# One PSUM bank moved from row maxima to scores in a self-attention loop

## The chip, the cores and the metric

The kernel runs on one core of a Trainium2 chip. The metric is the device time of one execution in microseconds (us), lower is better.

## What is computed

A decoder layer on `x` of 2 x 2048 x 512 in float32: self-attention with 16 heads of 32, then a cross-attention on a short context, then a mixture of eight experts, each with a residual and a layer norm. The change is in the self-attention:

```
qkv = x @ qkv_w + qkv_b                      # (2, 2048, 3, 16, 32)
attn = einsum('bnhd,bmhd->bhnm', q, k) * scale
attn = softmax(attn, axis=-1)
out = einsum('bhnm,bmhd->bnhd', attn, v) @ proj_w + proj_b
```

## The kernel before

The self-attention works on units (one batch and a group of four heads, 8 units) and in each on 4 chunks of 512 queries: 32 chunks. A chunk goes over 16 tiles of 128 keys (`kt`). For each key tile and head there is one *slot*: 64 per chunk, 2048 in all, with `CHUNKS` = 32, `T` = 16 and `HG` = 4 heads.

A slot has two matmuls on TensorE:

- the maxima pass (`max_pass`, L574): queries of the *next* chunk against 512 keys, one bank `mx` of 128 x 512. VectorE reduces it to a maximum per row (`reduce_max`, L463). The maxima of a chunk are ready before its scores start; the passes run 12 slots ahead beyond that.
- the score (`score`, L620): keys against the queries of this chunk, one bank `sc`. ScalarE makes the exponential of it (L426) into SBUF.

The order of the work is written out by hand for each engine, and semaphores hold the engines together. On TensorE a slot is always `max_pass`, then `score`:

```
for i in range(HG):
    n = (g + 1) * NMAX + LEAD + kt * PER_STEP + i
    if n < CHUNKS * NMAX:
        max_pass(n, n % NMAX, n // NMAX)
    score(g, kt, i)
    if i == 1 and kt % 2 == 0:
        burst(g, kt)
    if i == 2 and kt == T - EARLY and g + 1 < CHUNKS:
        transpose_shift(g + 1)
if (g, kt) in PART_AT:
    project_part(*PART_AT[g, kt])
```

`burst` is the products of probabilities with values (L589, `sa_pv`) of the two key tiles before, at every even key tile after its second slot, with the row sums (L597, `sa_den`) every fourth tile. `project_part` (L561, L565, `sa_misc`) is a piece of the next unit's projection, after key tiles 0 to 11. So TensorE's slots lie in runs: two slots, a piece of projection, the four slots of the odd key tile, a piece of projection, two slots, a burst. Without projection (tiles 12 to 15, and nearly everywhere in the last unit) eight slots follow each other between two bursts.

VectorE has, between the reductions and in its own written order, the reciprocals of the row sums (L490, at tiles 3 and 4), the leaving of a projection's result (L444, L455, L457, at tiles 4, 8 and 12), the shifts for the next chunk after tile 12 (`make_shift`: L468, L472, L474) and their leaving (L481) at tile 14, after TensorE has transposed them (L581) in tile 13. GpSimd adds the probabilities of four key tiles pairwise (L247), some 2.4 us each. The last chunk and the last 12 slots of the one before it have no maxima passes left.

PSUM has eight banks, all of them used here: two `sc`, three `mx`, and one each for `pv`, `den` and `misc`. The transposes at the start of the kernel also use `sc[0]` and `sc[1]`; that is not changed.

Of the kernel before, what the change touches and what calls it, by code (L numbers as in the profile page):

```python
# [10 lines left out]
ACT = mybir.ActivationFunctionType  # L11
AX_X = mybir.AxisListType.X

P = 128
BANK = 512
# [56 lines left out]
def self_attention(nc, z, x, xT_dram, qkv_w, qkv_b, attnT_dram, rows_dram):  # L72

    B, N, C, KC, G, HG, D, T, NQ = z.B, z.N, z.C, z.KC, z.G, z.HG, z.D, z.T, z.NQ
    SCALE = float(D) ** -0.5
    UNITS = B * G
    CHUNKS = UNITS * NQ
    QK = 3 * D
    AUG = QK + 2
# [66 lines left out]
    with ExitStack() as ctx:  # L146
        s = Stage(nc, ctx, "sa")
# [8 lines left out]
        q_stack = s.sb("q_stack", [P, HG, N], F32R)  # L156
        k_stack = s.sb("k_stack", [P, 2, HG, N], F32R)
        v = s.sb("v", [P, 2, T, P])
        prob = s.sb("prob", [P, 4, HG, BANK])
        part_max = s.sb("part_max", [P, TQ, HG, KQ])  # L160
# [6 lines left out]
        recip = s.sb("recip", [P, 2, BANK])  # L167
        empty = s.sb("empty", [P, W])

        sc = [s.ps(f"sc{i}") for i in range(2)]  # L170
        mx = [s.ps(f"mx{i}") for i in range(3)]
        pv = s.ps("pv")
        den = s.ps("den")
        misc = s.ps("misc")
# [12 lines left out]
        max_mm, max_read = s.sem("max_mm"), s.sem("max_read")  # L187
        top_ready, shift_hi, shift_ready = s.sem("top_ready"), s.sem("shift_hi"), s.sem("shift_ready")
        shift_mm, shiftT_ready, shift_in = s.sem("shift_mm"), s.sem("shiftT_ready"), s.sem("shift_in")
        sc_mm, prob_ready = s.sem("sc_mm"), s.sem("prob_ready")  # L190
# [11 lines left out]
        def after(engine, sem, value):  # L202

            if value > 0:
                engine.wait_ge(sem, value)
# [17 lines left out]
        @block.gpsimd  # L223
        def _(pool):
            make_ident(pool, ident, ident0, ident_ready)
            pool.wait_ge(ident_ready, 1)
            pool.memset(empty[:, :], 0.0).then_inc(made, 1)
            pool.wait_ge(made, 1)
            pool.memset(empty[:, C + 1:W].bitcast(I32), SKIP).then_inc(made, 1)
            for i in SPLITS:  # L230
                if JOBS[i].place is None:
                    move_stack(pool, i, (2, 3), stacked_too)

            def add_step(g, i, k):


                d = g * QUADS + i
                if k == 1:

                    after(pool, den_mm, d - 1)  # L240
                for half in range(2):
                    heads = slice(2 * half, 2 * half + 2)
                    pool.wait_ge(prob_ready, (g * T + 4 * i + k) * HG + 2 * half + 2)
                    if k > 1:
                        pool.wait_ge(quad_ready, d * ADDS + 2 * (k - 1) - 1 + half)
                    so_far = prob[:, 0, heads, :] if k == 1 else quad_sum[:, i % 2, heads, :]
                    pool.tensor_tensor(quad_sum[:, i % 2, heads, :], so_far, prob[:, k, heads, :], ALU.add).then_inc(quad_ready, 1)  # L247

            def divide(g):

                pool.wait_ge(sums_ready, g + 1)
                pool.wait_ge(recip_ready, TQ * (g + 1))
                pool.tensor_tensor(recip[:, g % 2, :], sums[:, :], recip[:, g % 2, :], ALU.mult).then_inc(attn_ready, 1)


            for i in (2, 3):
                pool.wait_ge(out_x[i], 2 * 16)
            for g in range(CHUNKS):
                for i in range(QUADS):
                    for k in range(1, 4):  # L260
                        add_step(g, i, k)
                        if (i, k) == DIVIDE_AT and g > 0:
                            divide(g - 1)
            divide(CHUNKS - 1)
# [88 lines left out]
        @block.scalar  # L353
        def _(act):

            def load_rows(chunk):
                act.dma_start(prob[:, chunk % NQ, :, :], x_v[chunk // NQ, chunk % NQ, :, :, :]).then_inc(in_rows[chunk % NQ], 16)

            def leave_transposes(chunk):

                b, n = chunk // NQ, chunk % NQ
                slot = xT[:, n % 2, :, :] if b == 0 else quad_sum[:, n % 2, :, :]
                if n >= 2:

                    act.wait_ge(out_x[2 * b + n % 2], 16)
                    if b == 0:
                        act.wait_ge(proj_mm, max(i for i, o in enumerate(FIRST_OPS) if o[1] == n - 2) + 1)
                for k in range(KC):
                    i = chunk * KC + k
                    act.wait_ge(tr_mm, i + 1)  # L370
                    act.activation(slot[:, k, :], sc[i % 2][:, :], ACT.Copy).then_inc(tr_read, 1)
                if b + 1 < B:
                    load_rows(chunk + NQ)
                act.wait_ge(tr_read, (chunk + 1) * KC)
                act.dma_start(xT_v[b, :, :, n * BANK:(n + 1) * BANK], slot).then_inc(out_x[2 * b + n % 2], 16)

            def leave_high(i):

                order = SPLITS.index(i)
                act.wait_ge(proj_mm, i + 1)  # L380
                if order >= 2:
                    before = JOBS[SPLITS[order - 2]]
                    stacked_first(act, before.what, before.n)
                bias = qkb[:, 0 if JOBS[i].what == "q" else 1, 0:1]
                act.activation(hilo[:, order % 2, 0, :], first_bank[i % 3][:, :], ACT.Identity, bias=bias).then_inc(hi_ready, 1)

            for chunk in range(NQ):
                load_rows(chunk)
            act.wait_ge(in_b, 16)
            for what, n in ALONE + sum(BETWEEN, []):  # L390
                if what == "t":
                    leave_transposes(n)
                elif what != "v":
                    leave_high(FIRST_OPS.index((what, n)))
            for i in range(4):
                act.wait_ge(out_x[i], 2 * 16)

            def leave_pv(g):

                act.wait_ge(pv_mm, (g + 1) * T)  # L400
                after(act, attn_ready, g)
                act.activation(sums[:, :], pv[:, :], ACT.Copy).then_inc(sums_ready, 1)

            def leave_den(g):

                act.wait_ge(den_mm, (g + 1) * QUADS)
                after(act, recip_ready, TQ * g)
                act.activation(dens[:, :], den[:, :], ACT.Copy).then_inc(dens_ready, 1)  # L408

            for g in range(CHUNKS):  # L410
                for kt in range(T):
                    step = g * T + kt
                    for j in range(HG):
                        n = step * HG + j
                        if j == 2 and kt == SUMS_AT and g > 0:
                            leave_pv(g - 1)
                        if j == 2 and kt == DENS_AT and g > 0:
                            leave_den(g - 1)
                        act.wait_ge(sc_mm, n + 1)

                        if j == 0:
                            after(act, pv_mm, step - 3)
                        if j % 2 == 0 and step >= 4:

                            act.wait_ge(quad_ready, (step // 4 - 1) * ADDS + 2 * max(kt % 4 - 1, 0) + j // 2 + 1)
                        act.activation(prob[:, kt % 4, j, :], sc[n % 2][:, :], ACT.Exp, scale=SCALE).then_inc(prob_ready, 1)  # L426
            leave_pv(CHUNKS - 1)
            leave_den(CHUNKS - 1)

        @block.vector  # L430
        def _(dve):
# [28 lines left out]
            def reduce_max(n, m):  # L460
                dve.wait_ge(max_mm, n + 1)
                q, j, k = m // (HG * KQ), m // KQ % HG, m % KQ
                dve.reduce_max(part_max[:, q, j, k:k + 1], mx[n % 3][:, :], AX_X).then_inc(max_read, 1)  # L463

            def make_shift(g):

# [35 lines left out]
            for m in range(2):  # L502
                reduce_max(NMAX + m, m)
# [4 lines left out]
            for g in range(CHUNKS):  # L508
                for kt in range(T):
                    for i in range(PER_STEP):  # L510
                        n = (g + 1) * NMAX + LEAD + kt * PER_STEP + i
# [14 lines left out]
        def _(pe):  # L526
# [41 lines left out]

            def max_pass(n, m, g):

                after(pe, max_read, n - 2)
                q, j, k = m // (HG * KQ), m // KQ % HG, m % KQ
                at = g % NQ * BANK + q * P
                pe.matmul(mx[n % 3][:, :], q_stack[0:QK, j, at:at + P], k_stack[0:QK, g // NQ % 2, j, k * BANK:(k + 1) * BANK],  # L574
                          start=True, stop=True).then_inc(max_mm, 1)

            def transpose_shift(g):
# [38 lines left out]

            def score(g, kt, j):
                n = (g * T + kt) * HG + j
                after(pe, prob_ready, n - 1)
                pe.matmul(sc[n % 2][:, :], k_stack[0:AUG, g // NQ % 2, j, kt * P:(kt + 1) * P],  # L620
                          q_stack[0:AUG, j, g % NQ * BANK:(g % NQ + 1) * BANK], start=True, stop=True).then_inc(sc_mm, 1)

            pe.wait_ge(ident_ready, 1)
# [25 lines left out]
            for g in range(CHUNKS):  # L649

                pe.wait_ge(shift_in, (g + 1) * 16 * HG)
                for kt in range(T):
# [7 lines left out]
                    for i in range(HG):  # L660
                        n = (g + 1) * NMAX + LEAD + kt * PER_STEP + i
# [1319 lines left out]
```

## Time and profile before

| | |
|---|---|
| median of 3 runs | 3720.26 us (3717.48 to 3720.76) |
| the profiled execution | 3720.95 us |
| its span, first to last instruction | 3719.2 us |
| busy in the span: TensorE matmuls | 3454.1 us (93%) |
| VectorE | 2508.9 us (67%) |
| ScalarE | 1671.8 us (45%) |
| GpSimd | 2053.2 us (55%) |
| mean granted TensorE clock | 0.958 of full |

The span is that of one profiled execution, and all rows are of it. Times in a timeline are from the start of the span. Matmuls are pipelined, and their ends are modelled, so a busy TensorE is not one at its peak: a wait can also stand ahead of a matmul's weight load (PEld), while the matmul before is still shown as busy. The loop over the chunks lies from about 110 to 2196 us of the span; the maxima passes end at 2110.

### The profile page before, as it was taken

What the parts mean: (1) busy time and instruction counts of PE and PEld (TensorE: products, weight loads), DVE (VectorE), ACT (ScalarE), POOL (GpSimd) and SP (SyncE); (2) the same over time, 40 slices, a digit from 0 to 9 for tenths busy, and PEclk for the clock granted to TensorE, in tenths of its full rate; (3) what the DMA queues carried; (4) which work ended last, traced back from release to release, by engine and by line L of the source; (5) the groups of instructions that cost most, each with busy time, mean ns of one, the idle gap of its engine ahead of it and who ended that gap; (6) DMA issues with size and microseconds to landing.
All of it is one profiled execution on the core that took longest, in us unless ns stands there. A gap on an engine that the chain in (4) does not pass through costs nothing. (4 is left out here: it accounts for less than half of the span.)

```text
span 3719.2 us, 50285 instructions
## 1 busy us (share of the span) xinstructions
PE 3454.1 (93%) x18109; PEld 2267.8 (61%) x18109; DVE 2508.9 (67%) x4510; ACT 1671.8 (45%) x3035; POOL 2053.2 (55%) x1025
## 2 busy tenths in 40 slices
PE   7999999999999999999999857999959999999996
PEld 5455455455455454554554325878849889988885
DVE  5777777777777777777777525778744665556667
ACT  2555555555555555555555533334312333223333
POOL 2689888888888888898888860011120011101111
PEclk9999999999999999999999878999969999999998
DMA  6321321312213122223210022122132243223333
GB/s 219 101 58 61 91 66 61 95 49 80 87 49 100 56 66 86 63 72 91 66 43 22 4 90 65 57 93 71 69 122 68 95 135 117 98 84 120 126 114 108
DMA packets 190274, 308.44 MB, mean 83 GB/s; under 512 B 25513, under 2 KB 72233, under 8 KB 190010
## 3 DMA queue, kind: packets, MB, share of 16 engines
q1 hardware_dynamic: 164330, 238.58, 20.6%
q0 software_dynamic: 14592, 44.32, 3.4%
q10 hardware_dynamic: 11088, 22.02, 1.7%
q8 instruction: 166, 2.72, 0.3%
q14 instruction: 98, 0.80, 0.1%
HBM read 195.66 MB, written 61.33 MB: 69 GB/s over the span
## 5 line engine op out<-in xcount | busy, mean ns | idle before, releaser
L463 DVE TENSOR_REDUCE sa_part_max<-sa_mx 128x1 f32<-128x512 f32 x2048 | 1281.6, 679 | 543.0 <-PE sa_mx L574 539.0
L426 ACT ACTIVATE sa_prob<-sa_sc 128x512 f32<-128x512 f32 x2048 | 1121.9, 595 | 823.3 <-PE sa_sc L620 780.5
L247 POOL TENSOR_TENSOR sa_quad_sum<-sa_quad_sum,sa_prob 128x1024 f32<-128x1024 f32 x512 | 1207.3, 2404 | 7.7 <-ACT sa_prob L426 7.7
L574 PE MATMUL sa_mx<-sa_k_stack,sa_q_stack 96*128 96x512 f32 x2048 | 967.0, 474 | 27.1 <-DVE sa_part_max L463 15.9
L620 PE MATMUL sa_sc<-sa_q_stack,sa_k_stack 98*128 98x512 f32 x2048 | 864.9, 424 | 8.2 <-ACT sa_prob L426 8.1
L247 POOL TENSOR_TENSOR sa_quad_sum<-sa_prob 128x1024 f32<-128x1024 f32 x256 | 616.3, 2431 | 257.5 <-ACT sa_prob L426 257.5
L574 PEld LDWEIGHTS sa_mx<-sa_k_stack,sa_q_stack 96*128 96x128 f32 x2048 | 389.5, 190 | 376.8 <-issue 205.5
L620 PEld LDWEIGHTS sa_sc<-sa_q_stack,sa_k_stack 98*128 98x128 f32 x2048 | 389.2, 190 | 318.7 <-ACT sa_prob L426 274.0
L1858 PE MATMUL ex_h<-ex_xT,ex_w 128*128 128x384 f32 (+2 forms) x2688 | 465.7, 329 | 41.6 <-issue 18.0
L589 PE MATMUL sa_pv<-sa_prob,sa_v 128*32 128x512 f32 x4096 | 502.8, 609 | 0.7 <-ACT sa_prob L426 0.7
L1858 PEld LDWEIGHTS ex_h<-ex_xT,ex_w 128*128 128x128 f32 x2688 | 447.7, 195 | 53.5 <-issue 25.4
L1869 PE MATMUL ex_acc<-ex_w,ex_hT 128*128 128x512 f32 x1728 | 418.2, 393 | 2.4 <-DVE ex_hT L1798 2.2
L1869 PEld LDWEIGHTS ex_acc<-ex_w,ex_hT 128*128 128x128 f32 x1728 | 319.1, 188 | 66.7 <-issue 4.9
L1676 POOL DMA_DIRECT2D ex_xg<-rows x48 | 26.5, 557 | 530.4 <-PE ex_h L1837 530.1
L1735 ACT ACTIVATE ex_h<-ex_h,ex_b 128x384 f32<-128x384 f32 x256 | 145.4, 581 | 373.5 <-PE ex_h L1858 373.5
L589 PEld LDWEIGHTS sa_pv<-sa_prob,sa_v 128*32 128x32 f32 x4096 | 108.1, 110 | 246.0 <-issue 241.6
L927 POOL TENSOR_TENSOR ca_rstd<-ca_var_eps,ca_minus_half 128x8 f32<-128x8 f32 x16 | 26.5, 1656 | 394.8 <-DVE ca_var_eps L1010 394.8
L1796 DVE CAST ex_hT<-ex_h 128x384 fp32r<-128x384 f32 x256 | 94.4, 369 | 147.8 <-ACT ex_h L1735 147.4
L1730 ACT ACTIVATE ex_w<-ex_w_in 128x512 fp32r<-128x512 f32 x128 | 80.6, 630 | 217.2 <-PE ex_acc L1869 217.2
L490 DVE RECIPROCAL sa_recip<-sa_dens 128x128 f32<-128x128 f32 x128 | 119.9, 941 | 77.4 <-ACT sa_dens L408 77.4
L1798 DVE TENSOR_TENSOR ex_hT<-ex_h,ex_hT 128x384 fp32r<-128x384 f32 x256 | 142.9, 558 | 8.9
L597 PE MATMUL sa_den<-sa_quad_sum,sa_ones 128*32 128x512 f32 x1024 | 135.4, 601 | 4.5 <-POOL sa_quad_sum L247 4.5
(199 smaller groups left out, 3186.4 us busy)
## 6 DMA issues: line engine op xcount, KB each, us to landing
ex_w_in<-in_L_ffn_w_dram SPq DMA_DIRECT2D x130, 512.0 KB, 4.4
sa_xT<-xT SPq DMA_DIRECT2D x57, 1024.0 KB, 5.1
sa_q_stack<-sa_hilo SPq DMA_DIRECT2D x372, 64.0 KB, 2.0
sa_k_stack<-sa_hilo SPq DMA_DIRECT2D x360, 64.0 KB, 2.0
rows<-sa_empty SPq DMA_DIRECT2D x48, 257.0 KB, 3.8
ex_rows<-rows POOLq DMA_DIRECT2D x8, 1542.0 KB, 7.4
ex_xg<-rows POOLq DMA_DIRECT2D x48, 256.0 KB, 3.0
sa_prob<-in_x_dram ACTq DMA_DIRECT2D x8, 1024.0 KB, 6.9
```

Source lines behind the costliest of these rows:

```text
L247: pool.tensor_tensor(quad_sum[:, i % 2, heads, :], so_far, prob[:, k, heads, :], ALU.add).then_inc(quad_ready, 1)
L426: act.activation(prob[:, kt % 4, j, :], sc[n % 2][:, :], ACT.Exp, scale=SCALE).then_inc(prob_ready, 1)
L463: dve.reduce_max(part_max[:, q, j, k:k + 1], mx[n % 3][:, :], AX_X).then_inc(max_read, 1)
L490: dve.reciprocal(recip[:, g % 2, cols], dens[:, cols]).then_inc(recip_ready, 1)
L574: pe.matmul(mx[n % 3][:, :], q_stack[0:QK, j, at:at + P], k_stack[0:QK, g // NQ % 2, j, k * BANK:(k + 1) * BANK], start=True, stop=True).t ...
L589: last = pe.matmul(pv[D * j:D * (j + 1), :], v[:, buf, kt, D * j:D * (j + 1)], prob[:, kt % 4, j, :], start=(kt == 0), stop=(kt == T - 1))
L597: last = pe.matmul(den[D * j:D * (j + 1), :], ones[:, :], quad_sum[:, d % 2, j, :], start=(d % QUADS == 0), stop=(d % QUADS == QUADS - 1))
L620: pe.matmul(sc[n % 2][:, :], k_stack[0:AUG, g // NQ % 2, j, kt * P:(kt + 1) * P], q_stack[0:AUG, j, g % NQ * BANK:(g % NQ + 1) * BANK], st ...
L1735: act.activation(h[:, j % 2, half * HALF:(half + 1) * HALF], h_bank[half][:, 0:HALF], ACT.Gelu, bias=b1[:, step:step + 1]).then_inc(h_read ...
L1798: dve.tensor_tensor(hT[:, j % 2, 1, cols], h[:, j % 2, cols], hT[:, j % 2, 0, cols].bitcast(F32), ALU.subtract).then_inc(hT_ready, 1)
L1858: last = pe.matmul(h_bank[half][:, 0:slots], w1[:, i % 2, pw, k, :], xT[:, e % 2, px, k, half * HALF:half * HALF + slots], start=(part == ...
L1869: last = pe.matmul(acc[t][:, :], hT[:, i % 2, ph, t * P:(t + 1) * P], w2[:, i % 2, pw, :], start=(i == 0 and part == 0), stop=(i == STEPS ...
```

## The change

One PSUM bank goes from the maxima to the scores: three `sc` and two `mx`. The indices and the two waits on TensorE follow from that: a score now waits until the exponential of the score three before it is done (it was two), and a maxima pass until the reduction of the pass two before it is done (it was three). The instructions and their order are the same on every engine; on TensorE the first three waits shift, because the first score that has to wait is the fourth and the first pass that has to wait is the third.

```diff
-        sc = [s.ps(f"sc{i}") for i in range(2)]
-        mx = [s.ps(f"mx{i}") for i in range(3)]
+        sc = [s.ps(f"sc{i}") for i in range(3)]
+        mx = [s.ps(f"mx{i}") for i in range(2)]
...
-                        act.activation(prob[:, kt % 4, j, :], sc[n % 2][:, :], ACT.Exp, scale=SCALE).then_inc(prob_ready, 1)
+                        act.activation(prob[:, kt % 4, j, :], sc[n % 3][:, :], ACT.Exp, scale=SCALE).then_inc(prob_ready, 1)
...
-                dve.reduce_max(part_max[:, q, j, k:k + 1], mx[n % 3][:, :], AX_X).then_inc(max_read, 1)
+                dve.reduce_max(part_max[:, q, j, k:k + 1], mx[n % 2][:, :], AX_X).then_inc(max_read, 1)
...
             def max_pass(n, m, g):
-                after(pe, max_read, n - 2)
+                after(pe, max_read, n - 1)
...
-                pe.matmul(mx[n % 3][:, :], q_stack[0:QK, j, at:at + P], k_stack[0:QK, g // NQ % 2, j, k * BANK:(k + 1) * BANK],
+                pe.matmul(mx[n % 2][:, :], q_stack[0:QK, j, at:at + P], k_stack[0:QK, g // NQ % 2, j, k * BANK:(k + 1) * BANK],
...
             def score(g, kt, j):
                 n = (g * T + kt) * HG + j
-                after(pe, prob_ready, n - 1)
-                pe.matmul(sc[n % 2][:, :], k_stack[0:AUG, g // NQ % 2, j, kt * P:(kt + 1) * P],
+                after(pe, prob_ready, n - 2)
+                pe.matmul(sc[n % 3][:, :], k_stack[0:AUG, g // NQ % 2, j, kt * P:(kt + 1) * P],
```

## Rows read from the trace of the kernel before

**Rows 1.** Costliest groups: busy us, mean ns | idle before, releaser
```profile
L463 DVE TENSOR_REDUCE sa_part_max<-sa_mx 128x1 f32<-128x512 f32 x2048 | 1281.6, 679 | 543.0 <-PE sa_mx L574 539.0
L426 ACT ACTIVATE sa_prob<-sa_sc 128x512 f32<-128x512 f32 x2048 | 1121.9, 595 | 823.3 <-PE sa_sc L620 780.5
```

**Rows 2.** Waits of TensorE's matmuls: us in total, times, longest
```profile
PE sa_mx L574 <- DVE sa_part_max L463: 15.9, 28, 0.8
...
PE sa_sc L620 <- ACT sa_prob L426: 8.1, 29, 0.5
```

**Rows 3.** Waits of TensorE's weight loads: us in total, times, longest
```profile
PEld sa_sc L620 <- ACT sa_prob L426: 274.0, 911, 1.0
...
PEld sa_mx L574 <- DVE sa_part_max L463: 122.3, 339, 1.1
```

**Rows 4.** Timeline, four-slot run, TensorE, VectorE, ScalarE: start us, us
```profile
830.08 0.40 PE L620 MATMUL sa_sc<-sa_q_stack,sa_k_stack 98*128 98x512 f32 x1
830.32 0.40 PE L574 MATMUL sa_mx<-sa_k_stack,sa_q_stack 96*128 96x512 f32 x1
...
830.78 0.39 PE L574 MATMUL sa_mx<-sa_k_stack,sa_q_stack 96*128 96x512 f32 x1
831.16 0.50 PE L620 MATMUL sa_sc<-sa_q_stack,sa_k_stack 98*128 98x512 f32 x1
831.50 0.40 PE L574 MATMUL sa_mx<-sa_k_stack,sa_q_stack 96*128 96x512 f32 x1
...
831.99 0.50 PE L561 MATMUL sa_misc<-sa_wkv,sa_xT 128*128 128x128 f32 x3
...
830.28 2.48 DVE L463 TENSOR_REDUCE sa_part_max<-sa_mx 128x1 f32<-128x512 f32 x4 [0.54 <-PE sa_mx L574]
...
830.51 2.27 ACT L426 ACTIVATE sa_prob<-sa_sc 128x512 f32<-128x512 f32 x4 [0.74 <-PE sa_sc L620]
```

**Rows 5.** Timeline, eight-slot run, tiles 14 to 0, TensorE and VectorE
```profile
821.35 0.50 PE L574 MATMUL sa_mx<-sa_k_stack,sa_q_stack 96*128 96x512 f32 x1
...
826.06 0.64 PE L589 MATMUL sa_pv<-sa_prob,sa_v 128*32 128x512 f32 x4
...
821.89 4.87 DVE L463 TENSOR_REDUCE sa_part_max<-sa_mx 128x1 f32<-128x512 f32 x8 [1.63 <-PE sa_mx L574]
```

**Rows 6.** Timeline, key tile 5 of a chunk, TensorE and VectorE
```profile
848.89 1.02 PE L565 MATMUL sa_misc<-sa_xT,sa_wq 128*128 128x512 f32 x2
...
847.64 1.81 DVE L463 TENSOR_REDUCE sa_part_max<-sa_mx 128x1 f32<-128x512 f32 x3
```

**Rows 7.** Timeline, key tiles 12 to 14, TensorE and VectorE
```profile
815.76 0.40 PE L574 MATMUL sa_mx<-sa_k_stack,sa_q_stack 96*128 96x512 f32 x1
...
816.45 0.60 PE L581 MATMUL sa_misc<-sa_ident,sa_shift 128*8 128x128 f32 x4
...
818.63 1.93 PE L589 MATMUL sa_pv<-sa_prob,sa_v 128*32 128x512 f32 x16
820.38 1.04 PE L597 MATMUL sa_den<-sa_quad_sum,sa_ones 128*32 128x512 f32 x8
...
815.99 3.07 DVE L463 TENSOR_REDUCE sa_part_max<-sa_mx 128x1 f32<-128x512 f32 x5
```

**Rows 8.** Busy time (instructions) by engine, then PEclk, DMA share, GB/s
```profile
120.00:1925.00 1805.00, 1785.78 (x9440) 922.51 (x9442) 1320.67 (x2136) 1004.57 (x1830) 1608.39 (x694) 1.00 0.24 72
2125.00:2160.00 35.00, 31.40 (x113) 9.91 (x113) 3.39 (x4) 18.65 (x36) 28.69 (x13) 0.71 0.02 8
```

**Rows 9.** L472 (ns min/median/max), and its timeline beside GpSimd and TensorE
```profile
L472 DVE TENSOR_SCALAR sa_shift<-sa_top x32: 175/176/4340, 99.1 to 2111.8; 128x16 fp32r<-128x16 f32 x32
...
1980.76 4.12 DVE L472 TENSOR_SCALAR sa_shift<-sa_top 128x16 fp32r<-128x16 f32 x1
...
1982.50 2.35 POOL L247 TENSOR_TENSOR sa_quad_sum<-sa_prob 128x1024 f32<-128x1024 f32 x1
...
1985.15 1.01 PE L581 MATMUL sa_misc<-sa_ident,sa_shift 128*8 128x128 f32 x4 [3.47 <-DVE sa_shift L474]
```

## The prediction

> **What bounds the kernel now.** I began with the costliest groups [rows 1]. The changed banks belong to the self-attention loop: 2048 passes for maxima and 2048 for scores on TensorE, 2048 reductions on VectorE, 2048 exponentials on ScalarE. The reader is to see the mean durations: a reduction takes 679 ns, an exponential 595 ns. Neither says who sets the pace; that is to be read from a timeline.
>
> Next the waits. TensorE's matmuls show hardly any: 15.9 us in total for a maxima bank and 8.1 us for a score bank [rows 2]. Read alone, that says that neither bank matters. But a matmul waits at its weight load, and the loads waited 274.0 us (911 times) for an exponential and 122.3 us (339 times) for a reduction [rows 3]. So banks do hold TensorE up, and the score bank does more often.
>
> How much of this is on the path is read from a run of slots in time (a slot is one maxima pass and one score). After a piece of projection, the four slots of an odd key tile follow [rows 4]. Unhindered, TensorE issues a matmul some 0.235 us after the one before (830.08, 830.32), so the run's first began at 829.85. The third score is late: it starts at 831.16, 0.05 after the first exponential ends (830.51 + 0.60 = 831.11), since only two score banks exist. The next matmul follows 0.34 after it and not 0.235, as its own weight load was not ahead. The run from 829.85 to 831.99 takes 2.14 us where eight issues would be 1.88, so the score banks cost 0.26. Yet VectorE in these four slots is busy without a gap: four reductions in 2.48 us, thus (2.48 - 0.68) / 3 = 0.60 apart, with 0.68 for one. The maxima pass of slot 4 (831.50) needs the reduction of slot 1 alone, as there are three banks.
>
> In runs of eight slots (key tiles 14, 15 and 0, without projection) the reductions go at (4.87 - 0.68) / 7 = 0.60 each as well [rows 5]. VectorE is therefore the slowest engine inside a run, and it catches up while TensorE does value products and projections. Three maxima banks are what lets TensorE leave a run before VectorE has finished it.
>
> **The change, part by part.** No instruction is added, removed or moved on any engine. Two waits change: score n waits for exponential n-3 in place of n-2, and maxima pass n for reduction n-2 in place of n-3.
>
> *The score side.* With three banks score 3 of a run no longer waits, so 0.26 per four-slot run could come back. But the maxima pass stands before its score in TensorE's order, so it has to come in time first.
>
> *The maxima side, four-slot run* [rows 4]. Reduction 1 ends at 830.28 + 0.68 = 830.96, reduction 2 at 830.88 + 0.68 = 831.56. Maxima pass 3 (now at 830.78) can start 0.05 after the former, 831.01, and score 3 at 831.35. Pass 4 needs reduction 2, 831.61, after that its score at about 831.90, and the projection at 832.15 to 832.2 in place of 831.99: **+0.2 us**. The wait for a score bank is gone and one for a maxima bank stands in its place, and the last slot now has a matmul more behind the wait. Such runs stand alone at key tiles 1, 7, 9 and 11 of each chunk: 4 x 0.2 = 0.8.
>
> *Key tiles 3 to 5.* Here VectorE has four reciprocals of 0.94 us and the projection's result between its reductions, and its queue sets the pace whatever TensorE does. TensorE left the run of tile 5 at 848.89, its last pass having waited for the reduction that ended at 848.27 [rows 6]. With two banks, that reduction lets the pass before it go (848.32), and the last waits for the next one: 848.24 + 0.68 = 848.92, score 849.26, projection 849.49. Against 848.89 that is **+0.6**, tile 3 included, since VectorE's queue is not later.
>
> *Tiles 12 to 14* [rows 7]. Two reductions, then the three small operations that make the shifts, then the others from 815.99. Pass 5 of the run needs reduction 3, which ends at 815.99 + 0.68 = 816.67, in place of reduction 2. It starts at 816.72 (now 815.76). Its score (817.07), the transposes of the shifts at 817.31 (now 816.45) and 0.44 of them, pass 6 at 817.75, pass 7 at 818.22 and pass 8 at 818.92 (reduction 6: 818.18 + 0.68, + 0.05) put the value products at 819.5 in place of 818.63: **+0.9**.
>
> *Tiles 14 to 0* [rows 5]. A late pass, to its reduction 0.54 (821.35 to 821.89), the reduction 0.68, to the next pass in that bank 0.05 to 0.06: 1.28 for two slots, 0.64 each in place of 0.60. Passes 2, 4, 6 and 8 then start at 821.92, 823.22, 824.50 and 825.78; score 8 at 826.12, value products at 826.36 in place of 826.06: **+0.3**.
>
> Sum per chunk 0.8 + 0.6 + 0.9 + 0.3 = 2.6 us; 31 chunks have maxima: **+80.6**. The last three have hardly any projections, so eight-slot runs (0.3) stand where 0.2 stood: +2. Before the loop twelve passes run at VectorE's pace, 12 x 0.04 = 0.5, say +1.
>
> *What comes back.* The last 76 slots have no maxima, and there the third score bank does what it is for. GpSimd's sums of pairs limit that gain: in 2125 to 2160 they leave 35 - 28.7 = 6.3 us [rows 8]. From 0 to 6.3 I take half: -3. And in the last chunks VectorE's operation L472 took 4.12 us in place of 0.18 because it began in the middle of a GpSimd addition; TensorE then stood 3.47 us [rows 9]. A slower TensorE lets GpSimd be less behind, so one of these three collisions may go: -3.5 (bounds: none, -11). By the Trainium skill, SBUF — State Buffer, section Who interferes with whom, a VectorE `tensor_scalar` and a GpSimd operation can hold a shared pair of ports against each other, the second blocked until the first ends. The trace agrees: the operation of 0.18 us ended only when GpSimd's additions did, at 1984.85.
>
> Sum: 80.6 + 2 + 1 - 3 - 3.5 = +77. The profiled execution took 3720.95 (span 3719.2), 0.7 above the median of the runs shown, so the median goes from 3720.3 to about **3798**. Bounds for a chunk: 2.0 if half of tile 12's loss is caught again by the value products' slack, 3.4 if stalls of neighbouring runs add up; that is +62 to +105, and with the last two terms at their ends 3776 to 3820.
>
> **Rivals.** *Faster: the third score bank wins.* For it: 911 waits of weight loads for exponentials against 339 for reductions [rows 3]. If TensorE could start pass 3 before reduction 1 has ended, by a reduction that starts earlier than 0.54 after its pass, the runs would fall to 1.88. It decides at 830.78: reduction 1 would have to end before 830.73, and it ends at 830.96. Price: five four-slot runs of 0.26 per chunk, -1.3 x 31 = -40, 3680. Against it: VectorE's 0.60 per slot. Chance 0.05.
>
> *No change.* A run's later end is taken up by slack behind it. That would need TensorE idle behind a run; instead TensorE is busy 1786 of 1805 us [rows 8], and the value products follow at once. 3720, chance 0.04.
>
> *Slower still: the clock.* In the trace the granted clock is 1.00 from 120 to 1925 and 0.71 from 2125 to 2160, with scores alone in TensorE's slots and after the longest L472, of 4.34 us [rows 8, 9]; that is, part of that stretch at 1.2 GHz and not 2.4. The value products and what follows before the next slot fill about 1.8 us (the unhindered issues of [rows 7], 818.63 to the sums at 820.38) and would take as long again at half clock; two such bursts a chunk would be 31 x 3.6 = +112 beside the +77, 3910. The new stalls are at most about 0.9 us where such a collision stops TensorE for over 3, which speaks against it. By the Trainium skill, TensorE: Matmul & The Clock Gate, section A second HAM failure mode: psum-queue depth-cycling, short idle times between groups of matmuls that cycle through banks made the clock swing between its levels. So far this trace disagrees: 911 such waits left it at 1.00. Chance 0.07.
>
> *Slower still: collisions.* L472 has been clear of GpSimd in 29 of 32 cases (median 0.176 us [rows 9]). If the shifted order brought it into an addition in every chunk, 28 x 3.5 = +98, 3896. It would run at the same place as now while GpSimd ends earlier or equally early, so chance 0.04.
>
> **How the numbers follow.** The forecast has 0.80. Its range 3776 to 3820 with the neighbours' chances outside it holds about 8 in 10. Faster and no change together have 0.09. A measurement of this kernel tells 0.2% (7.4 us) from nothing: faster 0.05, same 0.04, slower 0.91.
>
> **What would show it.** In the profile after: weight loads of scores that wait for exponentials nearly vanish, those of maxima passes that wait for reductions grow past 274 us in total; four-slot runs of 2.3 us; passes in one bank 1.28 apart in eight-slot runs; about 0.9 more from the first slot after the value products of tile 12 to those of tile 14; chunks some 2.6 longer; clock 1.00 in the loop; exponentials closer together in the last chunk. It is wrong if maxima passes start before the reduction two back has ended plus 0.05, if the clock falls in the loop, or if L472 grows in most chunks.

## The result and the profile after

| | before | changed |
|---|---|---|
| median | 3720.5 us (3717.5 to 3721.3, 4 runs) | 3791.2 us (3786.6 to 3796.7, 4 runs) |
| ratio | | 1.0195, 95% interval 1.0181 to 1.0209 |
| profiled execution: span | 3719.2 us | 3794.9 us |

The change costs 70.7 us; +77 was forecast. The profiled execution of the changed kernel is the slowest of its four. Its span is 75.7 us longer. Its self-attention ends 68.3 us later (GpSimd's last operation in it, L253, ends at 2271.9, before at 2203.7), and the other 7.4 us lie behind it, in code that did not change; among the kernels below whose banks for sums and products stay as they were, that part takes 1509 to 1523 us.

The weight loads' waits of the changed kernel (us in total, times, longest) have changed places against [rows 3]:

```profile
PEld sa_mx L574 <- DVE sa_part_max L463: 410.8, 917, 1.7
...
PEld sa_sc L620 <- ACT sa_prob L426: 61.7, 231, 0.8
```

Both halves are to be seen here: the wait for an exponential fell from 274.0 to 61.7, as the third bank promised, and the wait for a reduction rose from 122.3 to 410.8. The sum of the two went from 396 to 472 us.

A four-slot run of the changed kernel, TensorE and then VectorE, against [rows 4] (start us, us):

```profile
859.26 0.40 PE L620 MATMUL sa_sc<-sa_q_stack,sa_k_stack 98*128 98x512 f32 x1
859.50 0.40 PE L574 MATMUL sa_mx<-sa_k_stack,sa_q_stack 96*128 96x512 f32 x1
...
860.20 0.50 PE L574 MATMUL sa_mx<-sa_k_stack,sa_q_stack 96*128 96x512 f32 x1
860.54 0.40 PE L620 MATMUL sa_sc<-sa_q_stack,sa_k_stack 98*128 98x512 f32 x1
860.80 0.50 PE L574 MATMUL sa_mx<-sa_k_stack,sa_q_stack 96*128 96x512 f32 x1
...
861.37 0.61 PE L561 MATMUL sa_misc<-sa_wkv,sa_xT 128*128 128x128 f32 x4
...
859.46 2.57 DVE L463 TENSOR_REDUCE sa_part_max<-sa_mx 128x1 f32<-128x512 f32 x4 [0.54 <-PE sa_mx L574]
```

In this run scores now wait for nothing (860.54 is 0.34 after 860.20), and the maxima passes do: the third (the first stands at 859.03, beside the projection) starts at 860.20, 0.06 after the first reduction ends (859.46 + 0.68 = 860.14). In the whole trace no maxima pass starts less than 0.05 after the end of the reduction two before it. From that first pass (859.26 - 0.235 = 859.03) to the projection at 861.37 it is 2.34 us, before 2.14.

Tile 12 to tile 14 and on to tile 0 of the changed kernel, against [rows 7] and [rows 5]:

```profile
841.34 0.50 PE L574 MATMUL sa_mx<-sa_k_stack,sa_q_stack 96*128 96x512 f32 x1
...
844.57 0.50 PE L574 MATMUL sa_mx<-sa_k_stack,sa_q_stack 96*128 96x512 f32 x1 [0.61 <-DVE sa_part_max L463]
...
847.41 1.92 PE L589 MATMUL sa_pv<-sa_prob,sa_v 128*32 128x512 f32 x16
...
850.12 0.50 PE L574 MATMUL sa_mx<-sa_k_stack,sa_q_stack 96*128 96x512 f32 x1
...
852.01 0.50 PE L574 MATMUL sa_mx<-sa_k_stack,sa_q_stack 96*128 96x512 f32 x1
...
853.29 0.50 PE L574 MATMUL sa_mx<-sa_k_stack,sa_q_stack 96*128 96x512 f32 x1
...
855.23 1.07 PE L589 MATMUL sa_pv<-sa_prob,sa_v 128*32 128x512 f32 x8
...
843.83 1.97 DVE L463 TENSOR_REDUCE sa_part_max<-sa_mx 128x1 f32<-128x512 f32 x3
```

The first of these lines is the first pass after the value products of tile 12. In the kernel before it is:

```profile
813.50 0.50 PE L574 MATMUL sa_mx<-sa_k_stack,sa_q_stack 96*128 96x512 f32 x1
```

Pass 5 waits for the reduction behind the shift operations (843.83 + 0.68 = 844.51) and starts at 844.57; before, it did not wait for it. Passes 4 and 6 of the eight-slot run, in one bank, start 1.28 apart (852.01, 853.29). The run takes 5.11 us (850.12 to 855.23), before 4.71.

The collisions and the clock of the changed kernel, against [rows 9] and [rows 8]. First L472 (ns min/median/max), then the operation in chunk 28, then the loop's busy times:

```profile
L472 DVE TENSOR_SCALAR sa_shift<-sa_top x32: 176/177/719, 99.1 to 2191.9; 128x16 fp32r<-128x16 f32 x32
...
2061.34 0.66 DVE L472 TENSOR_SCALAR sa_shift<-sa_top 128x16 fp32r<-128x16 f32 x1
...
2059.56 2.40 POOL L247 TENSOR_TENSOR sa_quad_sum<-sa_quad_sum,sa_prob 128x1024 f32<-128x1024 f32 x1
2062.53 2.42 POOL L247 TENSOR_TENSOR sa_quad_sum<-sa_prob 128x1024 f32<-128x1024 f32 x1 [0.57 <-ACT sa_prob L426]
...
120.00:1925.00 1805.00, 1747.76 (x9028) 874.51 (x9028) 1291.48 (x2047) 988.77 (x1756) 1547.85 (x666) 1.00 0.23 69
```

No L472 is longer than 0.72 us, where three took 3.6 to 4.3. It still begins inside an addition (which ends at 2061.96), but GpSimd then waits 0.57 for an exponential, and the operation ends in that pause, at 2062.00. The clock in the loop stayed at 1.00 on average.

For all kernels, the length of a chunk is read from the starts of L481 (the copy of the transposed shifts; L488 in shift_on_scalar, last_five_banks and both_ends), once a chunk in tile 14: chunk 27 less chunk 1, by 26. The second and the fourth column are the last of these starts and the time from it to the end of GpSimd's last operation in the self-attention. Each row is one profiled execution.

| kernel (banks: scores, maxima) | L481 in chunk 27 | us per chunk | from there to the end |
|---|---|---|---|
| before (2, 3) | 1923.3 | 65.08 | 280.3 |
| changed (3, 2) | 1999.5 | 67.84 | 272.4 |
| two_two (2, 2) | 1997.2 | 67.73 | 271.5 |
| noden_two_three (2, 3) | 1923.1 | 65.01 | 280.5 |
| noden_three_two (3, 2) | 2003.0 | 67.87 | 270.3 |
| noden_three_three (3, 3) | 1883.1 | 63.58 | 270.2 |
| half_two_three (2, 3) | 1891.5 | 63.97 | 273.6 |
| half_three_two (3, 2) | 1853.3 | 62.50 | 269.1 |
| shift_on_scalar (2, 3) | 1928.7 | 65.30 | 279.5 |
| top_in_psum (2, 3) | 1924.2 | 65.06 | 262.0 |
| last_five_banks (2, 3) | 1922.4 | 65.01 | 273.1 |
| both_ends (2, 3) | 1922.1 | 65.03 | 256.0 |

The five kernels of two and three banks that do the same work up to chunk 27 (all of them but half_two_three and shift_on_scalar) lie within 0.07 us a chunk of each other; the part to the end repeats less well (270.3 and 272.4 with three and two). So the changed kernel loses 76.2 us up to there (28 chunks of 2.7) and gets 7.9 back behind.

### The profile page after: what moved, and what is told of

Read it like the earlier page. It is cut to its first block and busy times, and to the rows that moved or that the text cites. A ratio compares the mean times of both kernels' runs of the same rounds, so it can differ in the third digit from the quotient of the medians.

```text
span 3794.9 us, 50285 instructions
## 1 busy us (share of the span) xinstructions
PE 3493.2 (92%) x18109; PEld 2257.6 (59%) x18109; DVE 2532.8 (67%) x4510; ACT 1699.8 (45%) x3035; POOL 2058.2 (54%) x1025
## 5 line engine op out<-in xcount | busy, mean ns | idle before, releaser
L463 DVE TENSOR_REDUCE sa_part_max<-sa_mx 128x1 f32<-128x512 f32 x2048 | 1315.2, 683 | 597.5 <-PE sa_mx L574 594.5
L426 ACT ACTIVATE sa_prob<-sa_sc 128x512 f32<-128x512 f32 x2048 | 1149.7, 597 | 862.4 <-PE sa_sc L620 852.4
L574 PE MATMUL sa_mx<-sa_k_stack,sa_q_stack 96*128 96x512 f32 x2048 | 1022.2, 500 | 77.9 <-DVE sa_part_max L463 53.3
L620 PE MATMUL sa_sc<-sa_q_stack,sa_k_stack 98*128 98x512 f32 x2048 | 819.2, 402 | 2.2 <-ACT sa_prob L426 2.2
L574 PEld LDWEIGHTS sa_mx<-sa_k_stack,sa_q_stack 96*128 96x128 f32 x2048 | 387.1, 189 | 681.5 <-DVE sa_part_max L463 410.8
L620 PEld LDWEIGHTS sa_sc<-sa_q_stack,sa_k_stack 98*128 98x128 f32 x2048 | 390.7, 191 | 97.0 <-ACT sa_prob L426 61.7
## 6 DMA issues: line engine op xcount, KB each, us to landing
ex_xg<-rows POOLq DMA_DIRECT2D x48, 256.0 KB, 3.1
```

What stands on the lines that cost most here:

```text
L426: act.activation(prob[:, kt % 4, j, :], sc[n % 3][:, :], ACT.Exp, scale=SCALE).then_inc(prob_ready, 1)
L463: dve.reduce_max(part_max[:, q, j, k:k + 1], mx[n % 2][:, :], AX_X).then_inc(max_read, 1)
L574: pe.matmul(mx[n % 2][:, :], q_stack[0:QK, j, at:at + P], k_stack[0:QK, g // NQ % 2, j, k * BANK:(k + 1) * BANK], start=True, stop=True).t ...
L620: pe.matmul(sc[n % 3][:, :], k_stack[0:AUG, g // NQ % 2, j, kt * P:(kt + 1) * P], q_stack[0:AUG, j, g % NQ * BANK:(g % NQ + 1) * BANK], st ...
```

## The experiments

The theory was that the maxima bank taken away is the whole loss and the score bank is worth nothing beside two maxima banks; the rivals, that the score bank gives part of it back already, that something else than the reduction's cycle sets the pace, or that VectorE does so in any case.

**two_two** takes the third score bank away again, from the changed kernel:

```diff
-        sc = [s.ps(f"sc{i}") for i in range(3)]
+        sc = [s.ps(f"sc{i}") for i in range(2)]
...
-                after(pe, prob_ready, n - 2)
+                after(pe, prob_ready, n - 1)
```

(and `sc[n % 2]` in both places). 

> The changed kernel with the third score bank given back and left empty: two banks for scores, two for maxima. Theory (the maxima banks set the loss, the third score bank is idle beside two maxima banks while there are maxima passes): chunks 1 to 27 as long as in the changed kernel, 67.8 us on average against 65.1 before; only the end of the loop, with scores alone, loses what the third score bank gave there (chunks 30 and 31, some 5 to 9 us), so 3795 to 3801 us against 3791. Rival (the third score bank already takes back part of the loss in every chunk, by the third score of a run): 0.26 us more in each of five four-slot runs, 1.3 us a chunk, 3791 + 40 = 3831 us.

Measured: 3792.8 us (3783.9 to 3796.1), ratio to before 1.0200 (1.0186 to 1.0214), and 67.73 us a chunk. The changed kernel's ratio is 1.0195. The rival's 3831 is out. The end was not 5 to 9 us worse either, but the same (271.5 against 272.4), so the median lies 2 us below the range.

**noden_two_three, noden_three_two, noden_three_three** free a bank, so that three and three can be tried. They leave out the adding up of products and row sums over the key tiles, and their result is not the reference's; each ran once, and only the loop's chunks are read. The freed bank stays empty in the first two and is the third score bank beside three for maxima in the last. In all three:

```diff
-        den = s.ps("den")
+        den = pv
...
-                                     start=(kt == 0), stop=(kt == T - 1))
+                                     start=True, stop=True)
...
-                                     start=(d % QUADS == 0), stop=(d % QUADS == QUADS - 1))
+                                     start=True, stop=True)
...
+                if kt == 4:
+                    after(pe, dens_ready, g)
...
+            pe.wait_ge(sums_ready, CHUNKS)
```

> A control that frees a bank: the row sums' matmuls write to the bank of the value products, which then hold only the last product, so the attention's result is not the reference's and the experts get other tokens; only the self-attention loop is to be read. Two score banks and three for maxima, as before. All theories: chunks 1 to 27 as before, 65.1 us within 0.3.

> The same control with three score banks and two for maxima, as in the changed kernel. All theories: chunks 1 to 27 at 67.8 us within 0.3.

> The freed bank given to the scores beside three for maxima: three and three. Theory (the maxima bank taken away is the whole loss, and the score banks' waits are real where maxima do not hold TensorE up): the first and second score of a run wait for nothing, four-slot runs fall from 2.14 to about 1.9 us; chunks 1 to 27 at 63.6 to 64.0 us, 1.1 to 1.5 below the control with two and three and about 4 below that with three and two. Rival (VectorE at 0.60 a slot sets the pace of every run, so score banks are worth nothing even with three for maxima): 65.1 us.

The loop's chunks: 65.01, 67.87 and 63.58 us. The two controls repeat the kernel before and the changed one within 0.1, and three and three wins 1.4, where the rival had nothing. Its four-slot run has no wait left (TensorE, start us, us; the run's first pass is listed early at 821.71, beside the projection):

```profile
822.02 0.40 PE L622 MATMUL sa_sc<-sa_q_stack,sa_k_stack 98*128 98x512 f32 x1
...
823.66 0.50 PE L561 MATMUL sa_misc<-sa_wkv,sa_xT 128*128 128x128 f32 x3
```

Eight issues in 823.66 - (822.02 - 0.235) = 1.88 us. So the waits for score banks in [rows 3] were real, and a third bank for scores takes most of them away (in the whole trace 67.5 us are left of 274.0) and turns them into time, as long as the maxima keep three.

**half_three_two, half_two_three** shorten the reduction, with three and two and with two and three banks; they take the maxima of half of the keys. In half_three_two (in half_two_three it is `mx[n % 3]`):

```diff
-                dve.reduce_max(part_max[:, q, j, k:k + 1], mx[n % 2][:, :], AX_X).then_inc(max_read, 1)
+                dve.reduce_max(part_max[:, q, j, k:k + 1], mx[n % 2][:, 0:BANK // 2], AX_X).then_inc(max_read, 1)
```

> The changed kernel (three score banks, two for maxima) with every reduction over 256 of the 512 columns of its bank; the maxima are then those of half of the keys. A reduction should take about 0.42 us (between 0.22 for 64 columns and 0.68 for 512). Theory (the cycle 0.54 + reduction + 0.05 of a maxima bank sets the pace of a run): 1.01 us for two slots, close to what TensorE issues anyway (0.94), so the loss of 2.7 us a chunk vanishes and the score bank's gain shows: chunks at 62 to 63 us, 3630 to 3670 us. Rival (the loss comes from something else that goes with two maxima banks, such as weight loads that no longer run ahead): most of it stays, chunks at 66 to 67 us, 3760 to 3790 us.

> The kernel before (two score banks, three for maxima) with the same halved reductions. Theory: the score bank's cycle, 0.60 a slot, still holds the runs, so little is won: about 0.3 to 0.6 us a chunk at key tiles 3 to 5, where VectorE's queue is full; 3695 to 3715 us, and 40 us or more above the variant with three score banks. Rival (VectorE sets the pace of the runs before the change too, score banks do not matter): as fast as the variant with three score banks.

The reduction took 421 ns in both (costliest groups of half_three_two):

```profile
L463 DVE TENSOR_REDUCE sa_part_max<-sa_mx 128x1 f32<-128x256 f32 x2048 | 849.9, 421 | 885.7 <-PE sa_mx L574 816.6
```

Three and two: 3637.7 us (ratio 0.9779, 0.9764 to 0.9794), within its range and far from the rival's 3760 to 3790. Two and three: 3687.0 (0.9917, 0.9902 to 0.9932), 8 us lower than its range; its chunks get shorter by 1.1 us where 0.3 to 0.6 was expected, nearly all of it at tiles 4 and 5. The sign of the change turns: the bank move costs 70.7 us with reductions of 0.68 us and gains 49 with reductions of 0.42. That is the test of the cycle: 0.54 + 0.42 + 0.05 = 1.01 for two slots is near what TensorE issues in two slots, 0.94, and 1.28 is not.

**shift_on_scalar** and **top_in_psum** ask about the last chunks. The first gives L472's work to ScalarE:

```diff
+            def high_shift(g):
+                after(act, shift_mm, g)
+                act.wait_ge(top_ready, g + 1)
+                act.activation(shift[:, :, :, 0], top[:, :, :], ACT.Copy, scale=-1.0).then_inc(shift_hi, 1)
...
+                        if j == 1 and kt == T - EARLY and g + 1 < CHUNKS:
+                            high_shift(g + 1)
...
-                dve.tensor_scalar(shift[:, :, :, 0], top[:, :, :], -1.0, None, ALU.mult).then_inc(shift_hi, 1)
```

> The kernel before with the high part of the shifts (L472) made by ScalarE, so that no operation of VectorE with one SBUF input can wait for GpSimd's addition. Theory (in the last three chunks with maxima the 4.1 us of L472 and what follows it cost the kernel before 10 us or more, which the change got back by another timing): chunks 28 to 30 shorter by 2 to 5 us each, the others within 0.1 us, 3708 to 3716 us. Rival (the three collisions are hidden behind GpSimd's own queue, which is nearly full in these chunks): no change, 3719 to 3723 us.

Measured: 3730.9 us, ratio 1.0032 (1.002 to 1.0044), slower. The edit did not remove the collision; the operation behind it took it over (VectorE and GpSimd, chunk 28; L481 here is the old L474):

```profile
1988.11 2.99 DVE L481 SCALAR_TENSOR_TENSOR sa_shift<-sa_top,sa_shift 128x16 fp32r<-128x16 f32 x1 [0.69 <-ACT sa_shift L401]
...
1988.70 2.36 POOL L247 TENSOR_TENSOR sa_quad_sum<-sa_prob 128x1024 f32<-128x1024 f32 x1
```

It begins inside an addition that ends at 1988.77, and it ends at 1991.10, when the next one does (1991.06). The Trainium skill, SBUF — State Buffer, section Who interferes with whom, says that a VectorE instruction with two inputs in SBUF contends with a GpSimd one that reads SBUF; this trace agrees, 2.99 us in place of 0.18. Chunks are 0.2 longer besides (65.30). The 3708 to 3716 us expected were missed by 15. So this run decides nothing on the cost of the collision.

top_in_psum leaves both operations on VectorE and takes an SBUF input from each:

```diff
-        top = s.sb("top", [P, TQ, HG])
+        top = misc[:, 0:TQ * HG].rearrange("p (q j) -> p q j", q=TQ)
```

(and `top` for `top[:, :, :]` where it is written and read) 

> The kernel before (two score banks, three for maxima) with the 16 maxima per row (top) kept in 16 columns of the bank misc in place of SBUF, so that neither L472 nor L474 reads SBUF beside GpSimd's additions through more than one input. Theory (VectorE's shift operations waiting for GpSimd in the last three chunks, and the clock that falls after TensorE's stop, cost the kernel before some 13 us, which the changed kernel got back because its collisions last 0.7 us): no shift operation over 0.5 us, chunks 28 to 30 together 6 us or more shorter than 198.1, the part after the last maxima pass some 83 us in place of 92.7; 3702 to 3710 us. Rival (the collisions are hidden behind GpSimd's queue, and the changed kernel's short end comes from its longer stretch before): no change, 3717 to 3722 us. If the operand in PSUM does not free L472, the 4 us stay in it.

Measured: 3705.6 us, ratio 0.9959 (0.9945 to 0.9973). The operation is 0.18 us everywhere (ns min/median/max):

```profile
L472 DVE TENSOR_SCALAR sa_shift<-sa_misc x32: 174/175/176, 100.3 to 2104.1; 128x16 fp32r<-128x16 f32 x32
```

Chunks 1 to 27 stay at 65.06, and in the profiled executions 18.3 us are won behind them (280.3 to 262.0); by the medians it is 13.4 for the whole kernel, and 13 were expected. So the three collisions, some 12 us together as listed, cost that with what follows them. Part of what follows is the clock: in the kernel before the granted clock was 0.50 from 1983.5 to 1990.1, from 2051.8 to 2058.4 and from 2113.2 to 2123.2, each time 1 to 3 us after L472 had begun (1980.76, 2048.74, 2111.76). In the changed kernel it was 1.00 from 2060 to 2070, about its first long L472 (0.66 us), and 0.87 from 2127 to 2140, about its second. A stop is not needed for such a fall, though: in top_in_psum, without any, it was 0.50 from 1954.1 to 1960.7.

**last_five_banks** and **both_ends** give the last 76 scores all five banks, the second with top_in_psum's edit as well:

```diff
+        LAST = CHUNKS * NMAX - NMAX - LEAD
+
+        def score_bank(n):
+            return sc[n % 2] if n < LAST else (sc + mx)[(n - LAST) % 5]
+
+        def score_free(n):
+            return n - 1 if n < LAST + 2 else LAST if n < LAST + 5 else n - 4
...
+                after(pe, prob_ready, score_free(n))
+                if n == LAST + 2:
+                    pe.wait_ge(max_read, CHUNKS * NMAX)
```

(and `score_bank(n)` for `sc[n % 2]` in both places)

> The kernel before with the last 76 scores going round over five banks, the two of the scores and the three that the maxima no longer use. It tells what more score banks are worth where scores stand alone. Theory (GpSimd sets the pace there; the third score bank was worth only 1.3 us, as the changed kernel and its variant with two score banks differ): 0 to 5 us less, 3714 to 3720 us, the part after the last maxima pass 88 to 92 us. Rival (the score bank was what made the changed kernel's end short, 81 us in place of 92.7): 3705 to 3710 us.

> Both of these on the kernel before: top in PSUM and five banks for the last 76 scores. Theory: the sum of the two, 3700 to 3708 us, with the part after the last maxima pass at 81 to 83 us, where GpSimd never waits. Rival (one cause behind both): no better than the one of the two that wins.

Measured: 3710.6 us (0.9981, 0.9971 to 0.9991) and 3696.9 us (0.994, 0.9926 to 0.9954). The first is 3.4 us below its range and 0.6 above the rival's: where scores stand alone, more banks for them are worth much more than was held. The second is 3.1 below its range and 8.7 below the better of the two alone, so its rival, one cause behind both, is out. The windows from the first score without a maxima pass to the end (us, then busy time of TensorE, its weight loads, VectorE, ScalarE, GpSimd, then clock). The kernel before:

```profile
2111.00:2203.70 92.70, 70.35 (x288) 22.03 (x288) 12.58 (x13) 44.08 (x81) 75.69 (x34) 0.79 0.01 4
```

top_in_psum:

```profile
2103.30:2186.10 82.80, 62.81 (x288) 20.06 (x288) 8.47 (x13) 44.43 (x81) 74.89 (x34) 0.90 0.01 4
```

last_five_banks:

```profile
2110.90:2195.60 84.70, 53.48 (x288) 20.39 (x288) 12.67 (x13) 41.03 (x81) 75.86 (x34) 0.89 0.01 4
```

both_ends:

```profile
2097.00:2178.10 81.10, 52.24 (x288) 19.02 (x288) 8.45 (x13) 41.00 (x81) 74.89 (x34) 0.90 0.01 4
```

GpSimd works 75 us in each. At the end it waits 6.2 us for the last reciprocals (its last operation, L253, in the kernel before and in both_ends alike), and that makes a floor of 81. Either edit comes near it, so here they do not add: 9.9 and 8.0 alone, 11.6 together. The changed kernel takes 81.1 as well, with a clock of 0.85. Over the whole kernel the two still add up (13.4 and 8.4 by the medians, 22.1 together); both_ends is the fastest here that takes the maxima over all keys, faster than both kernels compared. Its profiled execution is also 4.2 us shorter than top_in_psum's between chunk 27 and this window, where the two kernels do the same. First top_in_psum, then both_ends:

```profile
1924.20:2103.30 179.10, 175.42 (x876) 78.72 (x868) 129.39 (x213) 105.82 (x193) 167.71 (x74) 0.97 0.05 14
...
1922.10:2097.00 174.90, 171.20 (x876) 77.21 (x868) 129.37 (x213) 105.95 (x193) 167.70 (x74) 1.00 0.05 15
```

VectorE, ScalarE and GpSimd work equally long; the same 876 matmuls are busy 4.2 us longer at a clock of 0.97. So this difference is the clock of one execution and not the edit (this execution of both_ends, at 3692.6 us, is the fastest of its six). The windows compared above can carry such a difference too, and a difference of less than about 5 us between two profiled executions says little in this part.

## Why the prediction was right, and where it was not

**What bounds the kernel.** Right. That the long wait on score banks is not what counts, and that three maxima banks let TensorE leave VectorE behind, is shown by two_two (nothing lost without the third score bank), by noden_three_three (1.4 us a chunk won with both) and by half_three_two (the loss turns into a gain when the reduction takes 0.42 us).

**Four-slot runs.** +0.2 forecast, +0.20 measured. Over chunks 1 to 27 the medians of tiles 1, 7, 9 and 11 grow by 0.21 each.

**Tiles 3 to 5.** +0.6 forecast; the mean lengths of the three tiles grow by 0.26, 0.19 and 0.24, 0.7.

**Tiles 12 to 14, and 14 to 0.** Value products to value products: 841.34 to 847.41 is 6.07 where 813.50 to 818.63 was 5.13, +0.94 (forecast 0.9), and 5.11 for 4.71, +0.4 (forecast 0.3). Sum 2.6 forecast, 2.76 measured.

**Before the loop.** +1 forecast, nothing measured. The passes did fall behind, the last of the twelve by 1.4 us (105.52 before, 106.96 now), but then TensorE waits for the transfer of the shifts into `sa_q_stack`, 2.96 us before and 1.48 now, and the first score starts at 109.8 in both.

**What comes back.** Mis-sized and wrongly divided. The terms for the last chunk and the collisions were -3 and -3.5, beside a loss in chunks 28 to 30 that went on at 2.6 and more. From L481 in chunk 27 to the end that comes to about +3; measured is -7.9. All three collisions shrank and not one, and one of them costs more than its own 3.5: top_in_psum wins 18.3 us without them. With 18.3 in place of both terms, beside the loss of some 10 that went on, the sum is -8. The 6.3 us that the prediction took as the room at the end were also only those from 2125 to 2160: over the whole end GpSimd is idle for 92.7 - 75.7 = 17.0 us, of which 6.2 (the wait for the last reciprocals) remain in both_ends too. The third score bank, taken for 3 us at the end, is not needed for that: two_two has two score banks, collisions gone too, and 271.5 us for this part against 272.4. So this term was 11 us off (+3 against -8), and up to chunk 27 the forecast was 2.4 us too low (28 x 2.6 + 1 = 73.8 against 76.2): 77 - 11 + 2.4 is the 68 us of the loop. The two errors have opposite signs, so the total is nearer than the term is, and that is luck; without it the forecast would still have held, as its range is 44 us wide.

**The sum and its range.** 3720.3 + 77 is 3797, not 3798. With the last two terms at their ends, +62 to +105 for the chunks and +3 for the rest give 3768 to 3828; the 3776 to 3820 of the prediction do not follow from its own bounds. 3791.2 lies within both.

**The rivals.** "The third score bank wins" failed at its own point of decision: no maxima pass starts before the reduction two back has ended. It holds where that reduction is short (half_three_two). No stall was absorbed in the loop's chunks, only the one before the loop. The clock did not fall with the new waits (1.00 on average from 120 to 1925), and no L472 took longer than 0.72 us.

## What to carry to other kernels

How long an engine waits for a bank is no measure of what a bank more is worth: here 911 waits stood for the scores and 339 for the maxima, yet the third bank of the maxima was worth 2.7 us a chunk, and a third bank for the scores nothing beside two for the maxima and 1.4 beside three, because another ring in the same order of issue held at nearly the same pace. Work out for each ring the cycle (issue to reader, reading time, release) divided by its banks, and compare it with what the issuing engine needs for as many slots; take a bank from the ring whose cycle stays below that, and none if none does. And when a kernel gets slower, look for what the slowness hides: the loss of 76 us was lightened by 8, mostly because three collisions shrank, and that gain can be had without the loss by moving 16 columns to PSUM.

## What the runs showed of the hardware that was not expected

- The reduction of 128 x 256 from PSUM takes 421 ns, that of 128 x 512 679 to 683 ns, and that of 128 x 64 from SBUF 220 ns.
- A small VectorE operation that meets GpSimd's queue waits until GpSimd itself pauses, not for the addition alone: 4.12 us in the kernel before, over the last 1.8 us of one addition and all of the next (2.35), and 6.84 us in half_three_two, where GpSimd was further behind. It holds for the form with one SBUF input (L472) and for the one with two; with the input in PSUM, neither waits.
- With the loop's order unchanged, the clock at the end went from 0.79 to 0.90 when the stops of 3.5 us were gone (top_in_psum), but also to 0.89 with the stops still there and five banks for the scores (last_five_banks; its three collisions last 3.6, 3.6 and 4.4 us). So the stops are not the whole cause; what it is stays open. In the changed kernel it was 0.85.
